# The attention values of a group of eight tiles planned as one piece instead of two halves

## The reference

```
x = layernorm(x + graph_convolution(x, adj))          # normalized adj @ (x @ weight) + bias
x = layernorm(x + attention(x, mask: adj == 0) ...)   # 8 heads of 32, projection, its own layer norm
x = layernorm(x + gru(x, adj))                        # 3 steps: adj @ h, gates z and r, candidate
x = layernorm(x + attention(x, mask: (1 - adj) * -1e9))
```

## Time and profile before

| | us |
|---|---|
| median of 3 runs | 2658.07 (2657.05 to 2658.81) |
| the profiled execution, its time | 2658.25 |
| its span | 2656.5 |
| TensorE busy (matmuls) | 2576.8 |
| VectorE busy | 1962.5 |
| ScalarE busy | 1904.9 |
| GpSimd busy | 715.1 |
| mean granted TensorE clock | 0.991 of full speed |

### The profile page before, as it was taken

How to read it: one execution, slowest core, us unless ns; L and a number is a source line. 1 busy time by engine, 2 the same in 40 slices (tenths; PEclk the granted TensorE clock), 3 DMA queues, 4 the chain that set the end, 5 groups by cost and what they waited for, 6 DMA issues and landing times.

```text
span 2656.5 us, 50191 instructions
## 1 busy us (share of the span) xinstructions
PE 2576.8 (97%) x17448; PEld 2056.3 (77%) x17448; DVE 1962.5 (74%) x5499; ACT 1904.9 (72%) x4284; POOL 715.1 (27%) x1065
## 2 busy tenths in 40 slices
PE   4999999999999999999999999999999999999997
PEld 3877877787877878778787787878777787777875
DVE  5867867868587786867768587685877868676776
ACT  2767947768587775858768587685867859574777
POOL 1222141322313222132322313223132321413221
PEclk7999999999999999999999999999999999999999
DMA  3312212122031221203122121221302113021122
GB/s 114 72 25 49 49 29 60 41 48 49 24 77 29 53 45 46 67 17 72 33 51 54 26 63 41 48 49 40 68 22 58 39 44 69 17 49 24 26 62 58
DMA packets 85081, 126.68 MB, mean 48 GB/s; under 512 B 15264, under 2 KB 34144, under 8 KB 84832
## 3 DMA queue, kind: packets, MB, share of 16 engines
q1 hardware_dynamic: 84832, 123.47, 19.7%
HBM read 14.36 MB, written 8.39 MB: 9 GB/s over the span
## 4 chain that ended last, share of the span: by engine, by line
PE 88%; DVE 6%; ACT 2%; issue 2%; POOL 1%; SPq 1%; DMA 0%; ACTq 0%; DVEq 0%; POOLq 0%
PE bank L1220 17%; PE bank L1222 17%; PE bank L1221 17%; PE bank L1279 15%; PE bank L1294 8%; PE bank L1271 8%; PE bank L1299 2%; PE bank L1262 2%; PE bank L1332 1%; PE bank L1239 1%; DVE probs L1028 1%; ACT probs L789 1%; SPq L616 1%; DVE PT L1039 1%; ACT PT L798 1%
## 5 line engine op out<-in xcount | busy, mean ns | idle before, releaser
L789 ACT ACTIVATE probs<-probs,few 128x512 f32<-128x512 f32 x1024 | 731.3, 718 | 90.1 <-DVE few L1028 86.5
L1028 DVE CUSTOM_DVE_ANT_0 probs<-bank,mask 128x512 f32<-128x512 f32 x1024 | 674.9, 683 | 61.0 <-PE bank L1279 26.0
L1279 PE MATMUL bank<-ident,probs 128*128 128x128 f32 x4096 | 588.6, 273 | 11.0 <-ACT probs L789 8.6
L1279 PEld LDWEIGHTS bank<-ident,probs 128*128 128x128 f32 x4096 | 483.9, 141 | 94.4 <-issue 25.4
L1271 PE MATMUL bank<-stack 96*128 96x512 f32 x1024 | 422.3, 453 | 0.7 <-DMA stack<-qk 0.5
L798 ACT ACTIVATE PT<-bank 128x512 f32<-128x512 f32 x640 | 360.0, 594 | 61.8 <-PE bank L1299 35.4
L1039 DVE COPY PT<-bank 128x512 f32<-128x512 f32 x384 | 262.8, 688 | 95.9 <-PE bank L1279 67.2
L709 POOL TENSOR_TENSOR feat<-o,feat 128x256 fp32r<-128x256 f32 x128 | 95.2, 744 | 632.7 <-ACT feat L811 614.8
L1220 PE MATMUL bank<-feat,W 128*128 128x512 f32 x640 | 258.6, 404 | 0.3
L1294 PE MATMUL bank<-PT,vh 128*32 128x256 f32 x4096 | 254.6, 383 | 2.5 <-DVE PT L1039 1.4
L1222 PE MATMUL bank<-feat,W 128*128 128x512 f32 x640 | 253.3, 396 | 0.0
(11 more groups left out here) (117 smaller groups left out, 5091.5 us busy)
## 6 DMA issues: line engine op xcount, KB each, us to landing
stack<-qk SPq DMA_DIRECT2D x768, 128.0 KB, 2.4
res<-in_x_dram SPq DMA_DIRECT2D x16, 512.0 KB, 3.8
out_dram<-res SPq DMA_DIRECT2D x16, 512.0 KB, 3.0
PT<-in_adj_dram SPq DMA_DIRECT2D x1, 1024.0 KB, 5.7
PT<-in_L_gnn_w_w_dram SPq DMA_DIRECT2D x2, 512.0 KB, 6.9
raw<-in_L_gnn_w_qkv_dram SPq DMA_DIRECT2D x1, 768.0 KB, 9.6
vh<-in_L_gnn_w_w_dram SPq DMA_DIRECT2D x1, 512.0 KB, 8.1
res<-in_L_gnn_u_w_dram SPq DMA_DIRECT2D x2, 256.0 KB, 8.1
```

The lines of the kernel that those rows point to most:

```text
L789: k = act.activation(p, p, ACT.Exp, bias=least[:, t % P_RING:t % P_RING + 1], scale=-1.0, accum_out=sums[:, grp % 2, q * HG + h:q * HG + h ...
L1028: k = dve.tensor_tensor_reduce(out=probs[:, t % P_RING, :], in0=place("scores", t)[:, :], in1=mask[:, half * QT + q, :], scale=1.0, scalar ...
L1279: k = pe.transpose(place("transpose", t)[:, m * P:(m + 1) * P], probs[:, t % P_RING, m * P:(m + 1) * P], ident[:, :])
```

## The change

PARTS becomes 1. Each group then has one values piece with a nominal duration of 1.86 us, with all 16 products and the factors' transposes, that waits for the eight pt pieces and for `rsum`. The instructions for a group and their semaphore waits stay as they are (`values`, line 1283, loops over all four key blocks in one call and waits for `rsum_ready` behind them), and the order on all engines is planned anew.

```diff
--- before
+++ after
@@ -24,7 +24,7 @@
 STACKED = 3
 SPARE = 8
 HI, LO = 0, 1
-PARTS = 2
+PARTS = 1
 
 
 class Signal:
```

## The result

The changed kernel takes 2695.43 us (2694.84 to 2695.83, 4 runs) against 2658.44 us: 37 us slower, ratio 1.0139, interval 1.0123 to 1.0155. The forecast was 2650 us and the range ended at 2668.

What follows compares the result with a forecast made beforehand. TensorE's list, in the planner's order, was taken as the bound. The terms -10.2 + 2 + 0 + 0 = -8.2 us took the 2658.25 us execution to a forecast of 2650 us (-0.31%), range 2635 to 2668.

Steps and rivals of the forecast that it cites:

- Step 1: On TensorE, 34 of 128 values groups no longer split by other work, 0.29 to 0.35 us each: 10.2 us saved.
- the sign that I gave for the gain: If the forecast was right, TensorE's busy time would be down by some 10 us.
- Step 2: The whole values piece waits for GpSimd's rsum factors, late in 31 groups: 0 to 25.4 us, taken as 2 us.
- Its sign of being wrong: TensorE's waits for PT copies or exponentials would grow beyond 20 us, just after values groups.
- Step 3: Work that stood between the halves comes later: 38 us at the end, taken as 0 since ScalarE and VectorE have free time.
- Step 4: New planned durations change the order in many places: 10 us less to 30 us more stalls, taken as 0.
- B: Attention chain becomes the bound through values waiting for GpSimd's factors, TensorE runs out of pieces: 2666 to 2673 us, chance 0.18.

Runs made afterwards that it cites:

- b_rsum_first: The kernel before, still two halves, but in the plan the first half too waits for the factors (rsum); 2647.89 us, ratio 0.9965.
- a_nominal_208: The changed kernel with the values piece planned at 2.08 us instead of 1.86; 2640.15 us, ratio 0.9936.
- b_glued: The kernel before in its old order, each split group's second half moved up directly behind its first on TensorE; 2677.40 us, ratio 1.0072.
- a_priority: The changed kernel planned anew, the second remainder of a new GRU state going first among ready VectorE pieces; 2663.13 us, ratio 1.0023.

## Why the prediction was wrong

- **What bounds the kernel.** Right: TensorE's list, in the planner's order.
- **Step 1, the price of a split.** Right in mechanism and size: -10.2 us forecast, -10.4 us measured as span less stalls (-10.0 in the other count, but only -4.9 if the median distance and not the quicker quarter is called normal). 127 of the 128 blocks take 1.87 us. Two details were wrong. Of the four splits counted as score products only one has a score; the other three have products of a GRU step. And the sign that I gave for the gain, a lower busy time, was wrong: busy counts the modelled tails, and short waits under them, so it rose by 10 us. What within a split costs the 0.3 us was not isolated.
- **Step 2, the wait for the factors.** The size, 2 us, matches the 2.0 us of the changed plan, but nothing in the runs isolates it. Its sign of being wrong did come: TensorE's waits for exponentials and PT copies rose from some 13 us to 35 us, behind values blocks. It did not tell what it was meant to tell, for the factors were no longer late: 3 groups start before theirs are ready, by 1.6 us in all, where there were 31 with 19.2 us. That the wait as such must cost is refuted by b_rsum_first and a_nominal_208, which have it and are faster than before.
- **Step 3, what stood between the halves comes later: taken as 0.** Wrong for a fixed order: b_glued lost 30 us in stalls, near the 38 us that I had written as the end of it. I argued with the free time of the other engines. But their lists are fixed too, and a free engine whose next piece is late does not help. In a plan made anew this loss need not appear, as a_nominal_208 shows.
- **Step 4, other planned durations: taken as 0 with -10 to +30 us.** This is the step that failed. The stalls rose by 47 us, beyond the upper end. I had taken the bounds from the spread between repeats of one plan, 0.6 to 8.4 us of visible idle time. Two things were wrong in this: visible idle time is only part of the stalls, and repeats of one plan are not a sample of plans. A plan can fall into a cycle of one graph, and then a hole is paid in every graph: starts came late by 0.5 + 1.0 + 0.2 + 0.8 + 0.6 = 3.1 us ten times at the first place and by 0.2 + 0.4 + 0.9 = 1.5 us 12 times at the second, together 49 us.
- **"What this does can't be worked out ... nothing shows a direction."** This premise of step 4 was wrong as well. The planner is Python and gives the new order before any run. The change moves the end of its plan from 2546.1 to 2572.4 us and TensorE's idle time in it from 42.3 to 96.7 us, 54 us more. With that in place of the 0, the sum would have come to some 46 us slower (-8.2 + 54.4); 37 us were measured.
- **The rivals.** B had the right side, and TensorE does run out of other pieces, but through the order, not through the factors. That the change would be slower got 0.19.

Five plans for the same whole blocks gave 2640 to 2695 us, while the change's own work is worth 10 us. Why the planner's rule (the piece that can start first) runs into the bad cycle at 1.86 and into a good one at 2.08 is not settled. Nor is it settled which sign the change has on average over plans: the five and a_priority have a median of 2671 us, the plans with two pieces (2658, 2665, 2653 with the same priority, 2648 with the wait moved, 2648 with the cut moved) lie lower, and these are few.

## What to carry to other kernels

Where a planner writes the order, a change of its input is two changes: the one meant, priced by the trace, and a new order. The second can be 55 us wide against a gain of 10, so its term must not be set to zero because it can't be worked out. Ask the plan first: the idle time of the bound engine in it costs nothing to compute, and here it gave the direction, nearly the size and the very places of the loss. It left 40 to 51 us between plan and trace, a spread of 11 us, so differences of a few microseconds between plans still have to be timed, with placebos (a nominal duration moved by a hundredth) to see the spread. Then make several plans and take the best: one of five was 0.6% faster than before. Moving single pieces by hand gave 4 us at best here and lost 38 us at worst.

## What the runs showed of the hardware

A pair of VectorE's `scalar_tensor_tensor` operations on 128x256 (line 1091) took 2.13 us where GpSimd worked beside it (changed kernel, in order of time):

```profile
1485.42 0.73 POOL L709 TENSOR_TENSOR feat<-o,feat 128x256 fp32r<-128x256 f32 x1
1485.73 2.13 DVE L1091 SCALAR_TENSOR_TENSOR vh<-vh,few,rows 128x256 f32<-128x256 f32 x2
1486.10 1.48 POOL L726 TENSOR_TENSOR feat<-vh,feat 128x512 fp32r<-128x512 f32 x1
```

In the kernel before the same pair took 0.88 us where GpSimd was idle:

```profile
1144.17 0.88 DVE L1091 SCALAR_TENSOR_TENSOR vh<-vh,few,rows 128x256 f32<-128x256 f32 x2
```

Over both traces, one operation of line 1091 took 0.47 to 0.48 us in all 34 cases without GpSimd work beside it, and 1.51 to 1.52 us in all 11 where GpSimd's 128x512 subtraction (line 726) ran, alone or with line 736. Beside GpSimd's operations on a few elements per partition (lines 680 to 694) it took 0.43 to 0.48 us in all 43 cases.
The Trainium skill, SBUF — State Buffer, Terms, has VectorE and GpSimd sharing a port pair under a lock. The rows beside the large GpSimd operations fit that, those beside the small ones show no price, and no run here took the GpSimd piece away.

The granted clock was 1.00, the 2.4 GHz level, in every repeat of both kernels, and 0.991 over the whole span in both, so nothing of the loss is clock.
